# Splitting the last four stores of a weight-selecting residual multiply into row pieces

## The reference

```
B, C, T = (64, 128, 2048)
W = weights[condition]
x = x + jnp.einsum('bct,bcd->bdt', x, W)
```

## Time and profile before

| what | value |
|---|---|
| median of three runs | 327.18 us (326.92 to 327.31) |
| span of the profiled execution, first to last instruction | 324.3 us |
| what the median has above that span | 2.9 us |
| DMA, mean over the span | 417 GB/s |
| PE busy | 71% of the span |
| DVE busy | 45% of the span |
| last load landed | 297.94 us after the start of the span |
| last sum done | 302.14 + 2.29 = 304.43 us |

### The profile page before, as it was taken

The page is one execution under the profiler, slowest core; times in us unless marked ns, Lnnn a source line. Parts: engine busy times, 40 slices in busy tenths (PEclk is TensorE's granted clock), DMA queues, the critical chain, the costliest instruction groups (busy, mean ns, idle before and its releaser), DMA issues.

```text
span 324.3 us, 2750 instructions
## 1 busy us (share of the span) xinstructions
PE 231.8 (71%) x512; PEld 94.7 (29%) x512; DVE 146.7 (45%) x64; ACT 0.2 (0%) x1; POOL 19.0 (6%) x69
## 2 busy tenths in 40 slices
PE   0039999999999867867768768678677687686200
PEld 0014444444444322322322323223223223232000
DVE  0005576676676554453553543534535535435200
ACT  0000000000000000000000000000000000000000
POOL 0010010010000000000000000000000000000000
PEclk9999999999999999999999999999999999999755
DMA  7999999999999999999999999999999999999995
GB/s 282 384 412 420 427 428 426 427 428 426 425 427 427 427 428 426 427 425 429 425 427 428 426 429 425 427 426 429 424 427 428 426 428 427 426 425 428 427 426 234
DMA packets 18962, 135.27 MB, mean 417 GB/s; under 512 B 2066, under 2 KB 2066, under 8 KB 2578
## 3 DMA queue, kind: packets, MB, share of 16 engines
q10 hardware_dynamic: 9746, 68.16, 49.9%
q1 hardware_dynamic: 9216, 67.11, 49.5%
HBM read 68.16 MB, written 67.11 MB: 417 GB/s over the span
## 4 chain that ended last, share of the span: by engine, by line
DMA 90%; PE 1%; SPq 1%; DVE 1%; issue 1%; DVEq 0%
DMA x_ring<-x 90%; PE product L105 1%; SPq L63 1%; DVE x_ring L127 1%; DVEq L127 0%
## 5 line engine op out<-in xcount | busy, mean ns | idle before, releaser
L105 PE MATMUL product<-x_ring,chosen_weights 128*128 (+1 forms) x512 | 231.8, 603 | 70.2 <-POOL chosen_weights L85 66.4
L127 DVE TENSOR_TENSOR x_ring<-product,x_ring 128x2048 f32 x64 | 146.7, 2292 | 157.8 <-PE product L105 157.8
L105 PEld LDWEIGHTS product<-x_ring,chosen_weights 128*128 128x128 f32 x512 | 94.7, 191 | 206.5 <-issue 206.4
L85 POOL COPY chosen_weights<-weight_table 128x128 f32 x64 | 18.8, 293 | 264.0 <-PE product L105 236.0
L140 ACT MOVE_SHAPE weight_table<-weights x1 | 0.2, 160 | 1.4 <-PEq L157 1.4
L157 POOL MEMSET const-float32-0.0<- 128x1 f32 x1 | 0.1, 98 | 0.1
L157 POOL MEMSET const-bfloat16-1.0<- 128x1 bf16 x1 | 0.1, 101 | 0.0
L157 POOL MEMSET const-uint8-127<- 128x1 uint8 x1 | 0.1, 101 | 0.0
L157 POOL MEMSET const-float32-1.0<- 128x1 f32 x1 | 0.1, 98 | 0.0
L157 POOL BASE_LOAD x1 | 0.0, 17 | 0.2 <-issue 0.2
## 6 DMA issues: line engine op xcount, KB each, us to landing
x_ring<-x SPq DMA_DIRECT2D x64, 1024.0 KB, 19.6
out<-x_ring ACTq DMA_DIRECT2D x64, 1024.0 KB, 19.5
condition_row<-condition ACTq DMA_DIRECT2D x1, 0.2 KB
weight_table<-weights ACTq DMA_DIRECT2D x1, 0.5 KB, 18.2
```

What stands on the lines that cost most here:

```text
L85: pool.tensor_copy(chosen_weights[u][:, :], weight_table[:, bass.ds(state * features, features)]).then_inc(weights_chosen, 1)
L105: last = pe.matmul(product[:, u % psum_slots, m * BANK_COLUMNS:(m + 1) * BANK_COLUMNS], chosen_weights[u][:, :], x_ring[:, bass.ds(ring_co ...
L127: dve.tensor_tensor(tile, product[:, u % psum_slots, :], tile, AluOpType.add).then_inc(sum_done, 1)
```

## The change

The turns of ACT's loop go from 1 to 14 instead of 1 to 15. The last turn is written out behind the loop. Its four stores wait for the same two semaphores as before, and each store is then issued as two or three DMAs over neighbouring rows of the same batch: 120 and 8 rows; 120, 6 and 2; 120, 4 and 4; 104 and 24. All pieces of a store raise the same semaphore by 16 each, and the final waits count them. Loads, multiplication and sums are as before, and so are the first 60 stores.

```diff
+LAST_ROWS = ((120, 8), (120, 6, 2), (120, 4, 4), (104, 24))
...
+        def last_column(u):
+            return ((turns - 1) % RING_TURNS) * (STEPS * time) + u * time
...
-            with act.Fori(1, turns) as turn:
+            with act.Fori(1, turns - 1) as turn:
                 for u in range(STEPS):
                     act.wait_ge(out_stored[u], 16 * turn)
                     store(turn, u)
-            for u in range(STEPS):
-                act.wait_ge(out_stored[u], 16 * turns)
+            for u, heights in enumerate(LAST_ROWS):
+                act.wait_ge(out_stored[u], 16 * (turns - 1))
+                act.wait_ge(sum_done, (turns - 1) * STEPS + u + 1)
+                row = 0
+                for h in heights:
+                    act.dma_start(out[(turns - 1) * STEPS + u, row:row + h, :],
+                                  x_ring[row:row + h, last_column(u):last_column(u) + time]
+                                  ).then_inc(out_stored[u], 16)
+                    row += h
+            for u, heights in enumerate(LAST_ROWS):
+                act.wait_ge(out_stored[u], 16 * (turns - 1 + len(heights)))
```

## The result

The changed kernel takes 332.27 us, the median of four runs from 328.48 to 334.30; the kernel before takes 327.09 us beside it. The ratio is 1.0129, with a 95% interval from 1.0080 to 1.0177: slower by 0.8 to 1.8%. The forecast was 326.7 us, no measurable change. Its range ended at 329.4. The runs of the changed kernel also lie 5.8 us apart, those of the kernel before 0.4 us. Ratios in this document leave out runs over 1.5% above the fastest of their kernel, here the longest (334.3) and in the run with four times 120 and 8 rows two of four (334.48 and 334.61); the granted clock of these runs is within 0.005 of the others', so they may belong to the kernel's own spread.

What follows compares the result with a forecast made beforehand. Bound by data movement, with one late DMA engine setting the end: removing its lag and adding 2.15 + 0.1 us to two others gave -0.4, with a quicker completion -0.5, so 327.18 became 326.7 us; range 325.9 to 329.4.

Steps and rivals of the forecast that it cites:

- What bounds the kernel: Whole kernel: bound by data movement; its end is set by DMA engines working off queued stores, one engine last.
- Which engine gets what: Last four stores: each piece uses the largest number of engines up to 16 dividing its rows, lowest-numbered first; 94 completions.
- Rival 4: Last four stores: 120 rows might use 8 engines with 15 rows each; +8.1 us, 335 us; chance 0.03.
- The sum: Tail of stores: late engine loses rows, two others gain 7 packets at 0.308 us each; -0.5 us in all.
- The straggler: The DMA engine ending last, at 323.3 us; taken as the sixteenth, or one losing rows (14 to 16).
- rival 1: Last four stores: the late engine is among those getting more rows; +0.9 to +2.3 us, up to 329.5; chance 0.14.
- ACT's own time: ACT's issuing of the last stores: six more issues cost nothing, or 3.3 us if their cover were gone.
- Rival 2: End of stores: the late engine's lag is absent or much smaller in timed runs; +2.2 us, 329.4; chance 0.13.
- Rival 3: Last four stores: the extra rows fall evenly over the engines; -1.8 us, 325.4 us; chance 0.08.

Runs made afterwards that it cites:

- the markers: Kernel before, with eight tiny loads of 2 to 15 rows queued behind its four whole last stores; 328.26 us, ratio 1.0047.
- column halves: Changed kernel with each of the last four stores as two DMAs of all 128 rows by half the columns; 326.53 us, ratio 0.9997.
- wide pieces alone: Changed kernel without the small pieces of the last four stores, leaving 120, 120, 120 and 104 rows; 332.19 us, ratio 1.0169.

## Why the prediction was wrong

**What bounds the kernel: right.** The kernel is bound by the DMA engines up to the end, one engine is late by about 2.5 us, and the change acts in the last 20 us alone.

**Which engine gets what: right.** The 30 further completions are those of the split that I read from 128 rows and from one, which is also the rule that the prediction takes from the Trainium skill ("DMA: Bandwidth & Descriptors", section "Why a DMA increments its semaphore by 16 and not by 1"). Rival 4 falls.

**The sum: wrong, in the price of a row.** The step that failed is "So the engines are not waiting for a shared resource here, and an idle neighbour makes none of them faster", and with it the 0.308 us that I put on every row. That price was measured with whole stores of 128 rows, in which no engine is seen to disturb another. I carried it to pieces of 120 rows, where a row costs 0.361 us between 314 and 320 us. The first half of the sentence was true of the rows it was read from and said nothing about the pieces. The prediction bounded the cost of a completion and of a one-packet piece, but not that of a data packet in a wide piece. It put the split at 2.25 us more for the two fullest engines and -0.5 us in all; measured are 5.2 us more by the medians.

The Trainium skill ("SBUF — State Buffer", section "Door 1: The DMA port swizzle") states that DMA reaches SBUF by 16 ports, that 4 neighbouring partitions share one, and that 32 partitions further the same ports come round again, so partitions 0 to 63 reach only eight. The runs agree in kind: 284 GB/s with 64 neighbouring rows, 423 with every second row. They don't give its 196 GB/s for 64 partitions; two halves were under way here, and whether that is the reason was not tested. Together with another page it would have given this as a rival before the run: the Trainium skill ("DMA: Bandwidth & Descriptors", section "The descriptor swizzle") has each engine at one port in a transfer to 128 partitions, and doesn't say that this holds for 120. The prediction doesn't set this against the change. The runs show which partitions matter; that the shared thing is the port is the page's explanation and not seen in a row.

**The straggler: wrong, and rival 1 right in its place, with too small a price.** The late engine is among those that get more rows, number 4 or 5 counted from 0, with 4 more; one engine alone for 2 us beyond 323.3 was the sign that the prediction gave for it. The changed kernel's own trace agrees with the markers. By the semaphores' events its last engine completes two pieces of the 120-and-8 store (319.57 and 320.60 us), two of the 120-6-2 store (323.19 and 323.73), one of the 120-4-4 store (326.19) and two of the 104-and-24 store (328.64 and 329.25). So it has part in the pieces of 8, 6 and 24 rows and not in those of 4 and 2.

Rival 1 priced four rows at +0.9 to +1.3 us, 328.2. The same events tell how much of the loss that is. From the issue of the last whole store to the last completion the changed kernel needs 24.96 us and the kernel before 19.38, 5.6 us more. Four rows at 0.308 are 1.2 us of it; the other 4.4 us are stretched packets. With 112 and 16 rows, where no engine has a row more, it is 24.18 us, 4.8 more, and with column halves 19.52. Of the engines 7 and 15 that the Trainium skill ("DMA: Bandwidth & Descriptors", section "Latency and other measured facts") calls usually slower, neither was the late one here; the page ties its guess at the reason to descriptors made by software, and the queues here are hardware ones (`hardware_dynamic`).

**ACT's own time: wrong.** I had six more issues at nothing, with 0.544 us as the highest price of one. They took up to 2.44 us. Where nothing collides, eight DMAs cost ACT less (column halves: 0.63 us in the median, last issue at 314.4), and they are free there. In the changed kernel the last wide piece goes out 2.57 us later than before. Some 1.8 us of that is the wait for the last whole store (landed at 315.83, before at 314.01), the rest ACT's own issuing, which went on to 316.73. None of it sets the end: the late engine's completion of the store before goes out at 325.85, so it takes up its rows of the last store 9 us after their issue. In the run with wide pieces alone, with four issues as before, the last issue was even 4.0 us late, from the late engine's completion and not from the number of issues.

**Rival 2** (the lag is a thing of the profile) falls: in every recorded run of the changed kernel the time is 1.7 to 2.1 us above the span, and 1.7 to 2.2 in those of the kernel before, so the spans grew with the times. The prediction's 2.9 us between span and median is larger than any of these; as it stands on both sides, it cancels in the difference. **Rival 3**, an early end by an even spread, isn't to be seen; the counts at the late engine, in this kernel and with the markers, are those of pieces that start at the same engine.

**Still open.** Why the runs of the changed kernel spread over 5.8 us while those with even and odd rows spread over 0.9: which engines meet depends on how far each has drifted, I would guess, and no run tested it. Also open is why number 4 or 5 is late at all, and whether it is the same on another chip. That the late engine of the run with wide pieces alone is the same one is assumed.

None of the splits of rows or columns beat the kernel before; at the best they equal it. No run tried to take rows off the late engine alone, since the row pieces to do it would be such as collide.

## What to carry to other kernels

A DMA of 128 partitions is more than the sum of its rows: a packet of it takes 0.308 us here, and in the tails with pieces of 120, 112, 104 or 64 neighbouring rows a packet took 0.36 to 0.46 us on average from 314 to 320 us. Who must split a store should split its columns, or take every second row, which cost nothing here. Before a per-row price is used for a new shape, ask which resource each engine had to itself in the shape it was measured in, and read the GB/s line beside the busy share, which can stay at 1.0 while a third of the rate is gone.

## What the runs showed that I had not expected

- One DMA engine of sixteen ends 2.5 to 2.9 us behind the others in the kernel before, at the fifth or sixth place; it is not the first or last. It falls back steadily: the last completion of a store comes 0.03 us after the fifteen others in the first turn and 2.6 us after them in the last, and grows by some 0.2 us a turn.
- A store is slowed by its successors: the last full store before the split ones completed late, and the next issue that waits for it came at 318.27 instead of 314.25. With 112 and 16 rows it shows in the DMA view from 304 to 305.5 us, in which this store is issued. Its landing time, the last number, before, with even and odd rows, and with 112 and 16:

```profile
out<-x_ring ACTq DMA_DIRECT2D x1, 1024.0 KB, 9.6
out<-x_ring ACTq DMA_DIRECT2D x1, 1024.0 KB, 9.6
out<-x_ring ACTq DMA_DIRECT2D x1, 1024.0 KB, 13.5
```

- Issuing a store took ACT 0.345 us in the kernel before, up to 1.2 us with eight column halves, and where packets were stretched up to 4.05 us (112 and 16 rows) and 3.0 us (64 neighbouring rows):

```profile
L158 ACTq DMA_DIRECT2D out<-x_ring x8: 566/1658/3019, 307.2 to 320.1; - x8
```

- Eight loads of 64 bytes a row behind the last store cost 1.5 us at the end, although they move 4.5 KB in all.
